# Finishing two tiles as a pair, with the small projections on 64x64 quarters of TensorE, in a four-layer pair-mixing kernel

## What is computed

```python
def layer(x_in):                                   # x_in = _gn(x), a group norm in 32 groups
    xn = layernorm(x_in) * norm_w + norm_b
    left  = (xn @ w_left  + b) * sigmoid(xn @ w_lgate + b) * mask    # mask in layers 0 and 2
    right = (xn @ w_right + b) * sigmoid(xn @ w_rgate + b) * mask
    out = einsum('bikh,bjkh->bijh', left, right)   # layers 1 and 3 contract the first axis instead
    og = sigmoid(xn @ w_ogate + b)
    # layers 0 and 1:
    return (layernorm(out) * ow + ob) * og @ w_out + bo
    # layers 2 and 3:
    return ((layernorm(out) * ow + ob) @ w_out + bo) * og
x = x + layer(_gn(x))                              # four times
```

## Time and profile before

| what | us |
|---|---|
| median of three runs | 2179.12 |
| lowest and highest run | 2172.59, 2180.49 |
| span of the profiled execution | 2173.6 |
| TensorE matmuls busy | 1889.5 (87%) |
| VectorE busy | 1692.2 (78%) |
| ScalarE busy | 1589.6 (73%) |
| GpSimd busy | 596.5 (27%) |

### The profile page before, as it was taken

The page is one execution under the profiler, slowest core; times in us unless marked ns, Lnnn a source line. Parts: engine busy times, 40 slices in busy tenths (PEclk is TensorE's granted clock), DMA queues, the critical chain, the costliest instruction groups (busy, mean ns, idle before and its releaser), DMA issues. The chain is left out here.

```text
span 2173.6 us, 44902 instructions
## 1 busy us (share of the span) xinstructions
PE 1889.5 (87%) x14485; PEld 1281.4 (59%) x14492; DVE 1692.2 (78%) x2690; ACT 1589.6 (73%) x2204; POOL 596.5 (27%) x574
## 2 busy tenths in 40 slices
PE   5686989789898998989988699899997979899998
PEld 4322968545422776855622498887552248778665
DVE  6787898989699767778968797787775977677664
ACT  3597878769798645658989685776888966576676
POOL 0000837355200000016500290651871000000755
PEclk8899999999999999989999899999999999999999
DMA  9599947279888928259989973936998984663897
GB/s 394 190 252 268 283 113 194 97 268 372 307 271 278 314 78 304 83 213 388 417 255 296 250 202 112 270 84 219 394 417 240 316 298 166 215 213 126 307 350 301
DMA packets 432439, 549.56 MB, mean 253 GB/s; under 512 B 17712, under 2 KB 329008, under 8 KB 415920
## 3 DMA queue, kind: packets, MB, share of 16 engines
q1 hardware_dynamic: 430720, 538.39, 74.4%
q10 hardware_dynamic: 1584, 9.51, 1.1%
HBM read 371.67 MB, written 176.16 MB: 252 GB/s over the span
## 5 line engine op out<-in xcount | busy, mean ns | idle before, releaser
L1617 POOL TENSOR_TENSOR LR<-LR 128x512 f32<-128x512 f32 x128 | 188.5, 1492 | 522.5 <-DVE LR L1663 499.0
L816 PE MATMUL bank<-whigh,kept 128*128 128x128 f16 x2048 | 271.5, 232 | 42.0 <-DMA kept<-XH 36.6
L816 PEld LDWEIGHTS bank<-whigh,kept 128*128 128x128 f16 x2048 | 263.3, 150 | 46.1 <-issue 37.7
L1608 POOL TENSOR_TENSOR LR<-LR,sum 128x2048 f32<-128x2048 f32 x30 | 136.6, 4552 | 528.6 <-DVE LR L1422 528.6
L816 PE MATMUL bank<-wlow,kept 128*128 128x128 f16 x2048 | 270.7, 232 | 0.0
L879 POOL TENSOR_TENSOR msgs<-sigs,mask_sb 128x256 f32<-128x256 f32 x192 | 124.9, 665 | 508.2 <-ACT sigs L853 501.8
L816 PEld LDWEIGHTS bank<-wlow,kept 128*128 128x128 f16 x2048 | 263.6, 150 | 0.0
L684 PE MATMUL bank<-LR,kst 128*128 128x512 f32 x512 | 254.9, 620 | 9.2 <-ACT LR L706 7.1
L1511 PEld LDWEIGHTS bank<-kst,LR 128*128 128x128 f32 x1024 | 151.1, 192 | 110.8 <-issue 91.0
L1523 PE MATMUL bank<-LR,wog 128*128 128x512 f16 x768 | 212.1, 386 | 4.8 <-ACT msgs L1564 4.0
L684 PEld LDWEIGHTS bank<-LR,kst 128*128 128x128 f32 x512 | 87.9, 192 | 180.9 <-issue 174.4
(11 more groups left out here) (189 smaller groups left out, 4130.6 us busy)
## 6 DMA issues: line engine op xcount, KB each, us to landing
kept<-XH SPq DMA_DIRECT2D x128, 512.0 KB, 5.5
LR<-XT SPq DMA_DIRECT2D x64, 1024.0 KB, 9.8
kept<-XHA SPq DMA_DIRECT2D x128, 512.0 KB, 4.9
XT<-LR SPq DMA_DIRECT2D x56, 1024.0 KB, 8.7
LR<-XT SPq DMA_DIRECT2D x78, 512.0 KB, 5.9
LR<-XH SPq DMA_DIRECT2D x64, 512.0 KB, 6.3
LR<-XHA SPq DMA_DIRECT2D x64, 512.0 KB, 5.9
OS<-kept SPq DMA_DIRECT2D x12, 2048.0 KB, 7.5
```

The source lines that it names most:

```text
L816: last = pe.matmul(bank(g)[:, j * P:(j + 1) * P], tokens(h, g // 4, g % 4, j, slice(0, P)), w[:, half * P:(half + 1) * P], start=part == 0 ...
L1608: pool.tensor_tensor(v, v, token(sum2, c, C), ALU.mult).then_inc(normalized.s, 1)
L1617: pool.tensor_tensor(by_b(x_of(c), q) if end else by_token_cols(x_of(c), q), by_token(gated[t % 4]), by_token_cols(xi[c % len(xi)], q), AL ...
```

## The change

**Layout.** A normalized chunk is laid out as (half, channel, side, 8 columns) instead of (side, channel, 16 columns). A turned tile then holds one side only, with the two halves of its 16 columns on partitions 0 to 63 and 64 to 127. Normalizing a chunk takes four VectorE operations of 512 elements per partition instead of two of 1024, and GpSimd's multiplication two of 1024 instead of one of 2048.

**Pairs.** Tiles t-1 and t (t odd) are the two sides of the same columns. `place(t)` gives the column group of a finished tile: 0, 2, 1, 3. At odd t `project_out` issues four 64x64 matmuls of 512 columns, one for each (side, half), from the pair's two tiles into banks 4 and 5, so that a bank again has both sides. It waits for both inputs and, by `taken.n + t - 1` with t odd, for both banks of the pair before to have been read. The even steps issue none. This holds in all four layers.

**Gate.** In layers 0 and 1 the gate is done at odd t for both tiles, by 12 matmuls of 64x64 with 512 columns (three passes for each of four quarters), into banks 2 and 3. `wog` and its parts of the weight folding are no longer made in these layers, and `load_xh` loads each part as two transfers of 64 partitions, one for each side. The lags of the programs stay as they are.

The core of the diff (semaphore totals and the unchanged parts of layers 2 and 3 are left out):

```diff
@@ load_xh @@
+                if layer["gate_first"]:
+                    for s in range(2):
+                        block = 2 * s + (part ^ s)
+                        sp.dma_start(buf[C * s:C * s + C, :], XH[ut, block, :, vb, :, :].rearrange("c g f -> c (g f)")
+                                     if layer["k_is_b"] else
+                                     XHA[block, :, ut, 16 * vb:16 * vb + 16, :].rearrange("c j a -> c (j a)")) \
+                            .then_inc(loaded_xh[c % 4].s, 16)
...
@@ rest (in fold) @@
+                if not late:
+                    return
...
@@ start (in fold) @@
-                dve.tensor_scalar(by_row(blast_gate), by_channel(K(K_LAST, C)), vec(V_NB, C), None, ALU.mult) \
-                    .then_inc(folded.s, 1)
-                dve.tensor_copy(by_row(drop_gate), by_channel(K(K_DROP, C))).then_inc(folded.s, 1)
-                dve.tensor_copy(by_row(last_gate), by_channel(K(K_LAST, C))).then_inc(folded.s, 1)
                 if late:
...
...
@@ token, wide @@
+        def token(t, c, h, channels):
+            v = t[:, ut, 0:N].rearrange("p (s v) -> p s v", s=2)[:, :, 16 * vb + 8 * h:16 * vb + 8 * h + 8]
+            return v.unsqueeze(1).broadcast_to([P, channels, 2, 8])
+
+        def upright(v, h):
+            return v.rearrange("p (h c s v) -> p h c s v", h=2, c=C, s=2)[:, h, :, :, :]
...
@@ normalize_chunk @@
-            dve.tensor_tensor(to[:, :, 0:HALF, :], of_chunk(0) if low else wide(homes.os[c % 4]),
-                              token(by, c, HALF), op).then_inc(done.s, 1)
-            dve.tensor_tensor(to[:, :, HALF:C, :], of_chunk(1), token(by, c, HALF), op).then_inc(done.s, 1)
+            for half in range(2):
+                for h in range(2):
+                    to = upright(homes.nrm[c % len(homes.nrm)], h)
+                    dve.tensor_tensor(to[:, HALF * half:HALF * half + HALF, :, :], of_chunk(half, h),
+                                      token(by, c, h, HALF), op).then_inc(done.s, 1)
...
@@ finish @@
+            def place(t):
+                return t // 4, (0, 2, 1, 3)[t % 4]
...
+            gate_w = halves_of_w[number % 2]
+            SIDES_HALVES = ((0, 0), (1, 0), (0, 1), (1, 1))
+            SIDES_HALVES_OUT = ((0, 0), (0, 1), (1, 0), (1, 1))
...
+                def out_gates(t):
+
+                    if t % 2 == 0:
+                        return
+                    c, e = t // 4, t % 4 // 2
+                    if e == 0:
+                        pe.wait_ge(loaded_xh[c % 4].s, loaded_xh[c % 4].n + 64 * (c // 4) + 64)
+                    pe.wait_ge(gate_ready.s, gate_ready.n + t - 1)
+                    for w, part in ((0, 0), (0, 1), (1, 0)):
+                        x = xh[c % len(xh)][part]
+                        for s, h in SIDES_HALVES:
+                            rows, q = slice(C * s, C * s + C), e + 2 * h
+                            last = pe.matmul(bank(2 + s)[C * h:C * h + C, :], gate_w[w][rows, 256:320],
+                                             pair_cols(x[rows, :], q) if k_is_b else by_b(x[rows, :], q),
+                                             start=(w, part) == (0, 0), stop=w == 1)
+                            if w == 1 and h == 1:
+                                last.then_inc(gate_projected.s, 1)
+
                 def project_out(t):
+
+                    if t % 2 == 0:
+                        return
                     pe.wait_ge(fed.s, fed.n + t + 1)
                     pe.wait_ge(taken.s, taken.n + t - 1)
-                    pe.matmul(bank(4 + t % 2), w_out, (gated if gate_first else aff)[t % 4],
-                              start=True, stop=True).then_inc(out_projected.s, 1)
+                    for side, h in SIDES_HALVES_OUT:
+                        rows = slice(C * h, C * h + C)
+                        last = pe.matmul(bank(4 + h)[C * side:C * side + C, :], w_out[rows, rows],
+                                         (gated if gate_first else aff)[(t - 1 + side) % 4][rows, :], start=True, stop=True)
+                        if side == 1:
+                            last.then_inc(out_projected.s, 1)
...
-                unrolled(tiles, (turn, 0), (out_gate, 0), (project_out, PO), *([(turn_back, TB)] if end else []))
+                unrolled(tiles, (turn, 0), (out_gates if gate_first else out_gate, 0), (project_out, PO), *([(turn_back, TB)] if end else []))
...
@@ normalize on GpSimd @@
-                    v = wide(nrm[c % len(nrm)])
-                    pool.tensor_tensor(v, v, token(sum2, c, C), ALU.mult).then_inc(normalized.s, 1)
+                    for h in range(2):
+                        v = upright(nrm[c % len(nrm)], h)
+                        pool.tensor_tensor(v, v, token(sum2, c, h, C), ALU.mult).then_inc(normalized.s, 1)
```

More of the change, by code:

```diff
@@ L340, in project_pe @@
             def project_pe(pe):
-                pe.wait_ge(folded.s, folded.n + (6 if late else 5))
-                for cols, drop, blast_, last_ in ((slice(0, 256), K(K_DROP, C), blast, K(K_LAST, 1)),
-                                                  (slice(256, 320), drop_gate, blast_gate, last_gate[0:1, :])):
+                pe.wait_ge(folded.s, folded.n + (6 if late else 2))
+                whole = ((slice(0, 320), K(K_DROP, C), blast, K(K_LAST, 1)),)
+                by_parts = ((slice(0, 256), K(K_DROP, C), blast, K(K_LAST, 1)),
+                            (slice(256, 320), drop_gate, blast_gate, last_gate[0:1, :]))
+                for cols, drop, blast_, last_ in by_parts if late else whole:
                     pe.matmul(projected_w[:, cols], drop, wfold[:, cols], start=True, stop=False)
@@ L414, in advance_fold @@
         def advance_fold(number):
-            advance((weights, 16), (folded, 5))
-            if not LAYERS[number]["gate_first"]:
-                advance((folded, 1), (late_folded, 3))
+            if LAYERS[number]["gate_first"]:
+                advance((weights, 14), (folded, 2))
+            else:
+                advance((weights, 16), (folded, 6), (late_folded, 3))
         ar = Arena(6 * COLS)
@@ L1604, in normalize @@
                     c = k + 1
-                    pool.wait_ge(mean_off.s, mean_off.n + 2 * c + 2)
+                    pool.wait_ge(mean_off.s, mean_off.n + 4 * c + 4)
                     pool.wait_ge(moment.s, moment.n + (8 if c < 8 else 8 + MOMENTS))
-                    v = wide(nrm[c % len(nrm)])
-                    pool.tensor_tensor(v, v, token(sum2, c, C), ALU.mult).then_inc(normalized.s, 1)
+                    for h in range(2):
+                        v = upright(nrm[c % len(nrm)], h)
+                        pool.tensor_tensor(v, v, token(sum2, c, h, C), ALU.mult).then_inc(normalized.s, 1)
                 def add(t):
-                    c, q = divmod(t, 4)
+                    c, q = place(t)
                     if q == 0:
@@ L1672, in finish @@
             for h in range(4):
[L1673 removed]
+                advance((landed[h], 0 if low else 4 * NCH), (loaded_xh[h], (16 if gate_first else 8) * NCH), (loaded_xt[h], 4 * NCH),
                         (stored[h], 4 * NCH))
```

58 lines of the change are left out of this document (30 added, 28 removed).

## The result

The changed kernel takes 2232.52 us (median of four runs, 2229.95 to 2233.01), beside 2178.57 for the kernel before (2172.59 to 2180.49): 1.0258 of it, interval 1.0238 to 1.0278. The range, 2187 to 2255, holds it, and so does the 0.77 on slower. The forecast was +36 and the result +54; a third of it was not foreseen, and more than a third of the loss in layers 0 and 1.

The account below looks back on a forecast made before the run. TensorE was taken to bound layers 0 and 1, with VectorE close behind. Terms +10.7 + 12.4 + 12.6 + 3 + 2 - 4 - 1 = +35.7 gave 2215 us by the median, range 2187 to 2255.

Parts of the forecast that it names:

- likeliest case: Whole kernel: the forecast itself, 2215 us by the median, chance 0.45, range of this case alone 2203 to 2235.
- pair wait and starts, layers 0 and 1: Finish stages of layers 0 and 1: VectorE waits for paired projections, +10.7 and +12.4, and later first projections, +3.
- clock: TensorE in layers 0 and 1: clock falls in not quite every second chunk, 1.0 us each, +12.6 together.
- loads by halves: Gate-input loads of 64 partitions in layers 0 and 1: no cost of their own, 0, bound +5.
- layer 2: Finish stage of layer 2: DMA sets the pace, no gain but in the first chunks, +2, bounds -5 and +10.
- layer 3: Finish stage of layer 3: TensorE's work shrinks but DMA caps the gain, -4, bounds 0 and -12.
- fold, ends, between stages: Weight folding of the layers that gate first loses small copies, -1 at most on the path.
- The wait that the change adds: Layers 0 and 1: VectorE stands 0.71 us per pair for the projection filling both banks; a chunk costs 8.90 us.
- The clock holds: Layers 0 and 1: TensorE never idle long enough for a fall, so the 12.6 goes: 2202; chance 0.25.
- Rival 2: Layers 0 and 1: clock at 1.2 GHz most of the time, 11.5 us per chunk, 2280; chance 0.10.
- Rival 3: Faster: no VectorE stall for the projection, 1.87 us per tile in layers 0 and 1, 2162; chance 0.10.
- Rival 4: Gate of layers 0 and 1: quarter matmuls don't overlap, 10 us per chunk, +40 more, 2255; chance 0.05.

Follow-up runs that it names:

- e6_rows_busy: Changed kernel with the gate-input loads of before and every fourth turn's transposes issued five times in layers 0 and 1; result not computed: 2203.17 us, 1.0123.
- e5_rows: Changed kernel with the gate's input of layers 0 and 1 loaded as before, two transfers of 512 KB; result not computed: 2239.14 us, 1.0282.
- e3_lags: Changed kernel with VectorE's gate and add one tile later in layers 0 and 1 (lags 8 and 10): 2216.58 us, 1.0193.
- e7_rows_lags: Changed kernel with VectorE's lags one larger and the gate-input loads of before in layers 0 and 1; result not computed: 2194.81 us, 1.0094.
- e2_busy: Changed kernel with the four transposes of every fourth turn of layers 0 and 1 issued five times over: 2217.26 us, 1.0182.
- e8_ggaa: Changed kernel with, in layers 0 and 1, VectorE doing two gates then two adds, 128x64 gate matmuls, loads and gate weights of before: 2220.39 us, 1.0206.
- e10_scalar_pairs: The version with paired VectorE order and 128x64 gates, plus ScalarE doing both scalings then both sigmoids in layers 0 and 1: 2189.38 us, 1.0056.

## Why the prediction was right, and where it was short

The direction and the mechanism of layers 0 and 1 came out. That the time lies inside the likeliest case too (2203 to 2235) is in part luck: the wait and the clock cost 25 us more than forecast, and layer 3 gave back 7 of them.

The sum in the terms of the prediction, against first-to-last sigmoids. The wait's own part is read from e6_rows_busy (clock up, loads of before), the clock's from e5_rows less e6_rows_busy. The last digits of the measured sum are rounded.

| term | predicted | measured | how |
|---|---|---|---|
| pair wait and starts, layers 0 and 1 | +26.1 | +35.3 | 146.9 + 154.2 - 265.8 |
| clock | +12.6 | +28.5 | 161.2 + 168.4 - 301.1 |
| loads by halves | 0 | -1 | 328.6 - 329.6 |
| layer 2 | +2 | +1.8 | |
| layer 3 | -4 | -10.7 | |
| fold, ends, between stages | -1 | +2.9 | |
| sum | +35.7 | +56.9 | |

**The wait that the change adds: right.** It was to be 0.71 in each pair and a chunk 8.90 us; with the clock up a chunk took 9.09. The bracketed waits are 0.74 and 0.49, and from start to start the two adds come 1.43 and 1.18 us after the gate before them, where VectorE alone would need 0.60: 0.83 and 0.58 more, 1.41 together against the 1.42 of the sum. VectorE's own work was right too (four small normalizing operations take 2.41, 2.40 taken). The missing 0.19 is one gate, 534.64, which starts 0.85 after its add instead of 0.67 and waits for ScalarE. The larger miss of this term is the chunk around the moments, still 13 us in e6_rows_busy, which I took to be nearly absorbed. One base was also misread: the window of layer 1 in the earlier trace rows starts at 970.0, where the turn of tile 5 is; that of tile 4 is at 965.20. Its 119.9 us are 4.8 too few. With the right base layer 1's term is +7.6 and the whole sum +31, so the forecast was nearer than its own working.

**The clock: the mechanism right, its rate wrong.** This is the term that was mis-sized. From the earlier trace rows I had idle times of 2.06 us without a fall and of 2.54 and 3.34 with one, found a gap of 3.1 in every chunk, and then wrote that I didn't expect a fall in every chunk. Nothing in the rows said so. The gap was 2.57 and the granted clock fell in nearly every chunk. One fall also costs more than the 1.0 taken: 10.3 less 9.1 is 1.2, as the turn and gate behind the slow projection run at the low level too. Fourteen falls of 1.2 in two layers make 34, and 28.5 were measured; the chunk around the moments takes some of them up, 11.8 us with falls (e5_rows) and 12.7 without (e6_rows_busy). 0.45 falls of 1.0 gave 12.6. The length of one gap was also the wrong thing to go by: 2.56 us passed without a fall once, and in e3_lags and e7_rows_lags the clock fell after gaps of 1.25. The runs do not give a rule for it. The Trainium skill (TensorE: Matmul & The Clock Gate, Part 1) had warned of such a swing, and in kind this trace agrees: 0.84 for a whole stage.

**Rivals.** "The clock holds" (2202) is what e6_rows_busy measured, 2203, so its condition was false and its time came out once the condition was made true. That too is partly luck, for layer 3's larger gain and the larger wait cancel; e2_busy, with the loads by halves, took 2217. Rival 2, the clock down most of the time, did not come: 0.84 in the mean, not near 0.5. Rival 3 fell with the 0.7 of waits. Rival 4 did too: the twelve float16 quarters of the gate go by in 0.77 us (553.99 to the next turn at 554.76), near the 0.65 taken. Its 2255 was also a little high by its own figures: 10 per chunk is 1.1 over 8.90, 32 us in two layers and not 40, so the upper end of the range rested on a slip.

**The signs.** The granted clock was below 0.98, chunks were over 8.9 and VectorE waited for the projection, as said. The waits were 0.6 to 0.8 in no pair of the shown chunk (1.64 and 0.20), and the projection's records took 1.99 in one pair of two. TensorE was busy 73% in layer 0, not 60%. And one sign of being wrong came, if "loses" is read as time off the stage: layer 3 went down by over 10 us.

**What the prediction did not see: ScalarE's side.** It looked at banks 4 and 5 and not at 2 and 3, which the pair's gate fills in the same way. In the changed order this costs little of its own (the 0.18 of the gate above; the 0.72 of the changed kernel come behind the slow projection). e8_ggaa and e10_scalar_pairs showed that it sets the pace as soon as VectorE's wait is taken away, at 1.2 us per chunk (9.16 against the mean of 7.7 and 8.2).

**DMA by halves: taken 0, and 0 as things stood**, for a reason that the prediction gave only in part. It cost nothing while the chunks were 10.3 us; at 9.1 or 8.3 it is 13 to 22 us. The bound of 5 was too low for a pace near the one predicted: at its own 8.90 us a chunk, the halves would likely have shown.

**Layer 2: the size right, by luck.** The prediction took its late chunks of 8.72 us to be DMA's. They take 8.23 after, at up to 419 GB/s. What that gains is lost in the chunk around the moments, 12.2 us by the turns' starts where it was 9.5. What ends that stall was not tried.

**Layer 3: right in sign, too small.** I let the DMA at 376 GB/s cap the gain. After, a window of the same stage moves 399, so 376 was not what the DMA could do; that it was what TensorE's pace asked for is my reading.

```profile
2150.00:2200.00 50.00, 49.91 (x352) 30.30 (x351) 43.25 (x48) 37.88 (x72) 32.18 (x23) 1.00 1.01 399
```

TensorE stays the bound, at 8.48 us per chunk (twice 4.24) and not the 7.9 of the plain sum. Fifteen chunks of 9.56 less 8.48 would be 16 us. The chunks around the moments keep 6 of them back: 11.3 and 14.1 us before, 15.5 and 13.7 after, 6.3 above their pace and then 12.3. From the pair's projection to the next matmul it is 1.02 (taken 0.9; a single tile's took 0.86), and from the last gate before it 0.74 (was 0.64). The Trainium skill (TensorEngine Tiling (Array Packing), Key Properties) states that changing the tiling mode drains TensorE. The estimate made from that in the prediction, 8.6 per chunk, was the better number for TensorE, and the rows agree with it within 0.12; the gain of 3 that it was to give was too small like the 4.

## What to carry to other kernels

- A matmul that fills two PSUM banks at once for two tiles takes the double buffering away on both: look at every engine that reads such banks, and ask what it has to do between its two reads. Here it became cheap only when both readers worked by pairs as well.
- If a change makes TensorE stand idle once in every turn of a loop, let one case of the sum have a fall of the clock in every turn, with what runs slowly behind it. A few single gaps in the trace of before do not say how often it falls. Work added beside the gap can shorten the kernel.
- "DMA engines busy 1.00" at a pace that another engine sets is no ceiling; take the highest rate that the trace shows for the same mix, and look at how many partitions each transfer covers.

## What was not expected of the hardware

- The granted clock fell once in nearly every chunk with 2.57 us of idle time, and in some chunks with 1.25: sixteen transposes more per chunk kept it up and brought a chunk from 10.3 to 9.1 us.
- With the gate's input in transfers of 64 partitions all DMA engines were busy at 302 GB/s, with 128 at 396; the median packet of 4096 bytes took 264 and 159 ns.
- A load of 512 KB written with an outermost index of two ran the DMA at a share of 0.49 and 168 GB/s with the stage waiting for it, 220 us in all over the changed kernel: two packets at a time in 0.47 of the window.
- The stalls of layers 2 and 3 grew with the change (chunks of 12.2, and of 15.5 and 13.7 us); they lie about where the second half's moments are made, and what ends them was not tried.
